# Retrieval scores: an earlier load of chunk 2, tile 0 stored by ScalarE, its copies ahead of late roundings, and three slots of tile 1 summed by TensorE

## The reference

```python
retrieved = mean(item_embeddings[indices], axis=1)             # 512 x 512
fused_input = concatenate([user_rep, retrieved], axis=1)       # 512 x 1024
fused_rep = fused_input @ W_fuse + b_fuse                      # 512 x 512
logits = fused_rep @ W_proj + b_proj                           # 512 x 12500
```

## Time and profile before

| | |
|---|---|
| median of three runs | 319.44 us (317.89 to 320.03) |
| the profiled execution | 319.95 us |
| its span in the trace | 317.9 us |
| mean granted clock of TensorE in it | 0.989 of full |
| TensorE busy | 298.8 us (94%) |
| VectorE, ScalarE, GpSimd busy | 248.4, 129.1, 83.8 us |

### The profile page before, as it was taken

How to read it: one execution, slowest core, us unless ns; L and a number is a source line. 1 busy time by engine, 2 the same in 40 slices (tenths; PEclk the granted TensorE clock), 3 DMA queues, 4 the chain that set the end, 5 groups by cost and what they waited for, 6 DMA issues and landing times.

```text
span 317.9 us, 4003 instructions
## 1 busy us (share of the span) xinstructions
PE 298.8 (94%) x1368; PEld 242.0 (76%) x1368; DVE 248.4 (78%) x354; ACT 129.1 (41%) x168; POOL 83.8 (26%) x84
## 2 busy tenths in 40 slices
PE   3968996989999999999999999999999999999995
PEld 1516874878879889888887888888888888888884
DVE  4899589894768883799869997979979798896123
ACT  1250436451002002325437665584556747563220
POOL 4778788876777710000000000000000000000000
PEclk9999996999999999999999999999999999999999
DMA  7995898989999621258728794948759296253315
GB/s 258 352 390 141 319 402 306 312 254 365 359 376 303 192 105 65 99 193 288 258 80 300 267 324 138 352 157 259 301 152 368 99 326 242 87 172 129 129 66 193
DMA packets 33348, 75.32 MB, mean 237 GB/s; under 512 B 5191, under 2 KB 21335, under 8 KB 33329
## 3 DMA queue, kind: packets, MB, share of 16 engines
q1 hardware_dynamic: 26416, 60.11, 52.9%
q0 software_dynamic: 6336, 13.92, 13.8%
q10 hardware_dynamic: 576, 1.05, 0.9%
HBM read 55.47 MB, written 25.60 MB: 255 GB/s over the span
## 4 chain that ended last, share of the span: by engine, by line
PE 67%; DVE 2%; issue 1%; ACT 0%; ACTq 0%
PE pair L1023 18%; PE pair L1082 15%; PE pair L1084 15%; PE pair L1085 15%; PE pair L1009 2%; DVE t_sums L811 0%; DVE early L813 0%; DVE w_lo L822 0%; PE pair L999 0%; ACT odd_sum L571 0%; DVE total L699 0%; DVE part_out L965 0%; DVE out_sb L766 0%; ACT w_hi L561 0%; ACTq L554 0%
## 5 line engine op out<-in xcount | busy, mean ns | idle before, releaser
L414 POOL DMA_INDIRECT ring<-item_embeddings,rows x68 | 71.7, 1054 | 23.8 <-issue 16.2
L1023 PE MATMUL pair<-w_hi,f_hi 128*128 128x500 f32 x144 | 57.3, 398 | 0.2
L1023 PE MATMUL pair<-w_lo,f_hi 128*128 128x500 f32 x144 | 57.2, 397 | 0.0
L1023 PE MATMUL pair<-w_hi,f_lo 128*128 128x500 f32 x144 | 57.0, 396 | 0.0
L1082 PE MATMUL pair<-w_hi,s_hi 128*128 128x500 f32 x128 | 49.8, 389 | 0.6 <-ACT odd_sum L571 0.6
L1084 PE MATMUL pair<-w_lo,s_hi 128*128 128x500 f32 x128 | 49.9, 390 | 0.0
L1085 PE MATMUL pair<-w_hi,s_lo 128*128 128x500 f32 x128 | 49.8, 389 | 0.0
L699 DVE SCALAR_TENSOR_TENSOR pair<-ring,mask,pair 128x512 f32<-128x512 f32 x56 | 42.1, 751 | 7.3 <-DMA ring<-item_embeddings,rows 4.1
L1084 PE MATMUL pair<-w_lo,f_hi 128*128 128x500 f32 x96 | 37.4, 390 | 0.0
L1082 PE MATMUL pair<-w_hi,f_hi 128*128 128x500 f32 x96 | 37.3, 389 | 0.0
L1085 PE MATMUL pair<-w_hi,f_lo 128*128 128x500 f32 x96 | 37.3, 388 | 0.0
(11 more groups left out here) (109 smaller groups left out, 416.8 us busy)
## 6 DMA issues: line engine op xcount, KB each, us to landing
w_raw<-w_proj SPq DMA_DIRECT2D x30, 500.0 KB, 7.7
logits<-part_out SPq DMA_DIRECT2D x21, 500.0 KB, 3.2
early<-w_proj SPq DMA_DIRECT2D x20, 500.0 KB, 5.6
logits<-out_sb SPq DMA_DIRECT2D x36, 250.0 KB, 3.7
logits<-out_sb SPq DMA_DIRECT2D x10, 500.0 KB, 3.0
early<-b_proj SPq DMA_DIRECT2D x8, 250.0 KB, 9.1
s_sum<-b_proj SPq DMA_DIRECT2D x8, 250.0 KB, 6.7
odd_bias<-b_proj SPq DMA_DIRECT2D x8, 250.0 KB, 5.9
```

The lines of the kernel that those rows point to most:

```text
L414: return nc.gpsimd.indirect_dma_start(out=to, out_offset=None, in_=table, in_offset=bass.IndirectOffsetOnAxis(ap=column, axis=0), **how)
L1023: m = nc.tensor.matmul(ps[:, 0:CHUNK], f[:, t, k, :], w, start=begin, stop=(f is f_lo and k == HK - 1))
```

## The change

SP loads chunk 2 as soon as the users' part is done, without waiting for slot 16 of tile 0, and stores nothing of tile 0. ScalarE stores each group of tile 0 after its own copy. Its copies of groups 0 to 3 stand each before a half rounding of chunk 4 or 5, those of groups 4 and 5 before chunks 6 and 7. Mean of tile 0 comes after the first half of chunk 2 and the fused rows after the first half of chunk 3. TensorE sums three slots of tile 1 instead of two (`PE_LAST`), and VectorE's total of tile 1 ends with slot 13. VectorE takes chunk 2 in one piece before its first add of tile 1 and does four adds after chunk 3.

```diff
-PE_LAST = 2
+PE_LAST = 3
...
             sp.wait_ge(user_fused, 1)
+            load_chunk(2)
             sp.wait_ge(slot_landed[place(0, PASSING - 1)], 16 * slot_uses(0, PASSING - 1))
-            for c in range(2, 6):
+            for c in range(3, 8):
                 load_chunk(c)
             for c in range(RESIDENT):
-                if c < 2:
-                    load_chunk(c + 6)
-                store(0, c)
                 if c == RESIDENT - 3:
                     sp.wait_ge(lo_ready, 8)
                 if c >= RESIDENT - 3:
+                    sp.wait_ge(first_evacuated, c + 1)
                     for b in range(3 * (c - RESIDENT + 3), min(3 * (c - RESIDENT + 4), BIAS_SLOTS)):
                         load_bias(b)
...
+            def store_first(c):
+                act.wait_ge(first_evacuated, c + 1)
+                act.dma_start(out_dram[0, :, c * CHUNK:(c + 1) * CHUNK], out_sb[:, c % OUT_SLOTS, :])\
+                  .then_inc(out_stored[c % OUT_SLOTS], 16)
...
             split_hi(1)
+            split_hi(2, (0,))
             mean(0)
-            split_hi(2, (0,))
+            split_hi(2, (1,))
+            split_hi(3, (0,))
             act.wait_ge(bf_landed, 16)
             fused_hi(0)
-            split_hi(2, (1,))
-            split_hi(3)
+            split_hi(3, (1,))
             for c in range(RESIDENT):
-                if c < 2:
-                    split_hi(c + 4)
...
                 if c < PE_LAST:
                     keep_last(c)
-                if c in (2, 3):
-                    split_hi(c + 4)
+                store_first(c)
+                if c < 4:
+                    split_hi(4 + c // 2, (c % 2,))
+                elif c < 6:
+                    split_hi(c + 2)
...
             add_last(1)
+            split_lo(2)
             add(1, 0)
             fused_lo(0, (0, 1))
-            split_lo(2, (0,))
+            split_lo(3, (0,))
             fused_lo(0, (2, 3))
-            split_lo(2, (1,))
-            add(1, 1)
-            split_lo(3, (0,))
-            add(1, 2)
             split_lo(3, (1,))
-            add_pair(1, 3)
+            for i in range(1, 5):
+                add(1, i)
             for t in range(TILES):
                 for c in range(RESIDENT):
                     if t + 1 < TILES and c < RESIDENT - 2:
-                        if AHEAD + 2 * c < last_add(t + 1):
-                            add_pair(t + 1, AHEAD + 2 * c)
+                        for i in range(AHEAD + 2 * c, min(AHEAD + 2 * c + 1, last_add(t + 1)) + 1):
+                            add(t + 1, i)
```

## The result

The changed kernel takes 319.93 us (median of 22 runs, 318.51 to 321.23) where the kernel before takes 318.40 (22 runs in the same rounds). The ratio is 1.0037 with a 95% interval of 1.002 to 1.0054: a loss of 0.4%, small and clear of noise. The three runs known ahead of the prediction had a median 1 us above that of the 22.

The account below looks back on a forecast made before the run. TensorE, busy 94%, was taken as the bound, with gather gates at 64.4 and 94.3 us behind its stalls. Of 5.8 us at group 3 only GpSimd's 1.1 us counted: 319.44 - 1.1 = 318.3 us, range 315.9 to 320.7.

Parts of the forecast that it names:

- nothing behind tile 2's sum changes: After the sum of tile 2, TensorE's work has no gap that the change closes or opens.
- VectorE's tail: VectorE's work between the landing of tile 2's lap and TensorE going on: 5.3 us, unchanged in length.
- The stall of group 3: TensorE's 3.1 us wait before group 3 of tile 0 goes; with the slow group after it, 5.8 us.
- The 1.1 us itself: Tile 2's home row lands sooner, so GpSimd's 1.57 us wait after it shrinks by 1.1 us: the whole gain.
- The failed step: Loading chunk 2 early delays tile 0's slots 13 to 16 by 0.5 us, bounds 0 and 6 us.
- the 3.9 us wait: TensorE's expected wait for slot 14 at tile 1's sum, said to cover even 3 us of delay.
- GpSimd's issue times up to 71.0 don't move: GpSimd issues its gathers, up to tile 2's home row at 71.00 us, at the same times as before.
- Three slots: TensorE sums one more slot of tile 1, about 1.0 us of matmuls; the added slot itself costs nothing.
- Stores on ScalarE: Eight store issues leave SP, costing ScalarE 0.46 us each, 3.7 us in all; it fits and gains no bandwidth.
- A: Rival: gathers land quicker in a thinned stretch, tile 2's gate up to 3.8 us sooner; 316.7 us; chance 0.25.
- B: Rival: the wait at tile 1's sum slows TensorE's clock, tile 2's sum starts later; 320.3 us; chance 0.2.
- C: Rival: stores on a third queue delay tile 1's slots 13 to 16 by up to 1.3 us; 319.4 us; chance 0.1.

Follow-up runs that it names:

- sum_tile2: Kernel of late_sp_c, with TensorE also summing slots 14 to 16 of tile 2: 320.25 us, ratio 1.0042 to the kernel before.
- rep_before: The kernel before the change, run once more unchanged: ratio 0.9988.
- rep_after: The changed kernel, run once more unchanged: ratio 1.0018 to the kernel before.
- late_chunk2: Changed kernel with chunk 2 loaded behind slot 16's landing again, ScalarE's and VectorE's order up to the first projection as before: 318.38 us, ratio 0.9999.
- half_early: Changed kernel with only the first half of chunk 2 loaded ahead of the wait for slot 16: 318.27 us, ratio 0.9985.
- early_alone: Kernel before, with only chunk 2's load moved ahead of the wait for slot 16: 321.55 us, ratio 1.0119.
- home_p2_b: late_chunk2 with home and lap gathers two slots later in tiles 1 to 3: 320.95 us, ratio 1.0064; the same kernel on another chip (home_p2): 0.9919.
- home_m2_b: late_chunk2 with home and lap gathers two slots sooner in tiles 1 to 3: 318.52 us, ratio 0.9993.
- late_sp_b: late_chunk2 with tile 0's stores issued by SP again: 318.10 us, ratio 0.9977.
- late_sp_c: Same kernel as late_sp_b, late_chunk2 with tile 0's stores on SP, run once more: 318.35 us, ratio 0.9981.

## Why the prediction was wrong

**What sets the end.** The forecast's claim that nothing behind tile 2's sum changes held in every trace of the chips near 318 us but sum_tile2's, which adds work there. The start of that sum, the span, and the landing of tile 2's lap (issue time plus time to landing):

| kernel | lap landed | sum of tile 2 starts | idle before it | span | span less start |
|---|---|---|---|---|---|
| before | 88.9 | 94.41 | 0.66 | 317.9 | 223.5 |
| rep_before | 87.6 | 93.43 | none | 316.8 | 223.4 |
| changed | 88.4 | 93.78 | 0.35 | 317.2 | 223.4 |
| rep_after | 87.8 | 93.18 | 1.16 | 316.6 | 223.4 |
| late_chunk2 | 86.6 | 92.07 | 1.42 | 315.4 | 223.3 |
| half_early | 87.5 | 92.92 | 0.70 | 316.3 | 223.4 |
| early_alone | 91.0 | 96.48 | 0.50 | 319.9 | 223.4 |
| home_p2_b | 91.3 | 96.72 | 2.08 | 320.1 | 223.4 |
| home_m2_b | 83.7 | 92.98 | none | 316.5 | 223.5 |
| late_sp_b | 86.9 | 92.29 | 0.99 | 315.7 | 223.4 |
| late_sp_c | 87.3 | 92.75 | 0.48 | 316.1 | 223.4 |

Wherever TensorE waited, it started 5.4 to 5.5 us behind the lap's landing. That is VectorE's tail of the forecast (5.3). The two traces of the changed kernel (88.4, 87.8) lie between the two of before (88.9, 87.6): the loss of its timed runs is in neither of them.

**The stall of group 3** went with its slow group, as forecast, in the changed kernel and in late_chunk2. **Its worth** was forecast as 1.1 us of 5.8; by the timed runs of late_chunk2 it is nothing (0.9999, half-width 0.27%, which is 0.9 us). The rest is covered by gather traffic: at tile 1's sum TensorE waits 1.45 us for slots, at tile 2's 1.42 for the total. The 1.1 us itself was GpSimd's wait for tile 2's home row, 1.57 us in the trace. In late_chunk2 the home row landed at 76.9 instead of 79.2, but rep_before's, with no change at all, landed at 77.5, and GpSimd waited only 0.30 us behind it. So the whole gain of the forecast was read off a wait of one execution, a long one of its kernel, and by these runs there was nothing to win.

**The failed step** behind the loss is "I take 0.5 us, since late slots bring few rows and 1 MB is gone in 2.5 us. Even 3 us would be covered by the 3.9 us wait". Slot 13 landed 3.4 us later, TensorE idled 4.2 us, its clock halved, and the first projection was 5.0 us late; in rep_after these were 1.4 us, 1.8 and 0.8 us, no slow clock, and 2.3 us. All of it is above 0.5 and inside the bound of 6 that the text gave. Few rows did not make the gather quick beside the load. The nearest row was the 8.2 us beside loads, and I chose the other one. Even so 3 us would have been harmless: half_early, at 3.5 us, loses nothing. What was wrong beside the size is "GpSimd's issue times up to 71.0 don't move". I let the delay act on TensorE alone. Through VectorE's adds it can hold ring slots, and so GpSimd, which feeds the gate. early_alone shows this path: 4.3 us of such waits, the home row 2.8 to 3.0 us later, the lap landed at 91.0 and TensorE going on at 96.48. It is not hidden by TensorE's wait; it lengthens it. For the changed kernel the path is argued only. Its trace has 4.1 us of such waits, but rep_before has 2.1 and rep_after none, and its home row went out at 71.59 and 71.00.

That the load costs time, and that it suffices, is shown by the timed runs: putting it in alone costs 1.2%, taking it out (with the order up to the first projection) brings the time back, and so does taking out half of it with nothing else changed (0.9985). Why the loss is 0.4% in the changed kernel and 1.2% in early_alone is argued only: there ScalarE's copies come behind two halves again, and group 6 (63.72) waits 1.97 us for the copy of group 3, which stands behind both halves of chunk 6.

**Three slots** at tile 1 were never taken back alone near 318 us; that they cost nothing there rests on the waits for slots at that sum (1.45 us in late_chunk2, 2.20 in rep_after) and on half_early's time. sum_tile2 shows that the same step costs 2.9 us where TensorE does not wait. **Stores on ScalarE** took 0.35 us each to issue instead of 0.46 and delayed nothing visibly (the copy at 46.20, the store at 46.81 for group 0).

**The rivals.** A (quick gathers) did not occur: the lap still took 8.6 us. B's mechanism, a wait that brings the clock to 1.2 GHz, occurred, but before slot 13 and not at tile 1's sum, a place that the text did not name. Its 320.3 us is near the measured 319.93, but by a route that it did not describe. C did not show: slot 16 of tile 1 lands at 63.1 to 63.8 with the stores on ScalarE, inside the 62.6 to 64.5 of those with them on SP, and with the stores on SP the time is 0.2% lower, unresolved. The Trainium skill (DMA: Bandwidth & Descriptors, "Queues, rings and completion order") says that each engine serves its queues in turn, packet by packet. I used it against the store's third queue, and it speaks as much about the second, the load against tile 0's gathers: 3.3 us to land became 6.7 with one load beside it (4.7 in rep_after). The trace agrees as far as that goes; it does not show in what order the packets went.

**The number.** The range (315.9 to 320.7) held the time, and the sign was wrong. That it held is in part luck: the forecast started from 319.44, the median of three runs, and 22 runs gave 318.40. From there the same steps give 317.3 us and a range up to 319.7, which misses.

## What to carry to other kernels

A gap in the DMA's work is free only if nobody waits for the small transfers that travel in it. Before filling it, see whose landing ends the wait behind it, and price that landing by the rows beside a load, not by those in the gap. When a cover is claimed for a delay, follow the delay on every engine that it reaches, also through the buffers that a late reader gives back late. And before removing a stall, find the next two gates and the time that TensorE itself needs up to them: here both ended within a microsecond of each other. A wait of about a microsecond in one trace should be looked up in a second trace before a gain is built on it.

## What the runs showed of the hardware that I had not expected

TensorE's clock was at 0.50 after a shorter wait than the 3.1 us of the earlier trace rows: in half_early after 2.53 us without a matmul, where the next 16 took 3.50 us instead of 2.02. In rep_after, with 1.84 and 0.82 us of waits close together, it stayed at full. At tile 1's sum it was at 0.50 after 2.22 us in home_p2_b (16 matmuls in 3.23 us), and after 1.36 and 0.44 us in home_m2_b, but at full after 2.20 us in rep_after (24 in 2.92). So in these traces the length of the last wait alone does not tell whether the clock falls.

The same kernel took 318 to 319 us on three chips and 336 and 339 on two others. The kernel of home_p2 lost 0.64% on one of the first (1.0064, interval from 1.0032) and gained 0.8% on one of the others (0.9919, interval up to 0.998). A ratio below 1% that was measured on one chip need not carry to the next.
